# Destinations of the expert rows made by POOL, one instruction a tile, in a routed-expert kernel

## The chip, the cores and the metric

The kernel runs on one core of one Trainium2 chip. The metric is the device time of one launch in microseconds. Three runs of the kernel before gave 370.55, 370.05 and 370.35 us, a median of 370.35 us.

## What is computed

Four residual layers act on `x` (4 x 512 tokens of 128 values): a cross-attention to a small context, a layer of eight experts that each pick tokens, a second cross-attention, and a gated layer of eight SwiGLU experts with a shared expert beside them. The change is in the last one:

```
logits = normed @ router_w.T
top_v, top_i = top_k(softmax(logits), 2)          # two experts a token
gates = softmax(top_v)
out = sum over e of comb[:, e] * swiglu(normed, gate_up_w[e], down_w[e])
out = out + swiglu(normed, shared_gate_up_w, shared_down_w)
```

Each of the 2048 tokens goes to two different experts: 4096 rows of expert output.

## The kernel before, in words

**Sending.** When the router has chosen, POOL scatters each token's row twice into the DRAM table `dispatched_rows` (`send_rows`, L783 to L788, 32 indirect DMAs of 128 rows), once into the region of each of its two experts. A row is the normed token as high and low float16 halves, and three more words (L952, L953, L1016): word D is twice the token's number, word D+1 is its first expert, word D+2 is 0. SP writes pad rows behind the last row of each region: word D is 4096 + p (p is the partition), D+1 is -1, D+2 is 1.

**Tiles.** DVE plans 40 tiles of 128 slots. An expert takes as many tiles as its rows fill, the last one filled up with pad rows; tiles that no expert needs read the region of pads alone. So 40 x 128 = 5120 slots hold 4096 rows and 1024 pads. As the eight experts can need at most 39 tiles, the last tile holds pads only. `te` holds each tile's expert.

**The loop over tiles** is software-pipelined over PE, ACT, DVE, POOL and SP. At step s (`step_pe`, L1453; `step_act`, L669; `step_dve`, L1093):

- SP (`load_slots`, L471) loads tile n's rows into `slot_rows` (`xd`), a ring of four: the load of tile n waits until tile n-4 has been transposed (`rows_turned`) and until the destinations of tile n-4 have been taken out of its rows (`dest_ready`).
- PE transposes the rows of tile s+4 (L1462), multiplies tile s+3 with the gate and up weights (L1160, from `slot_rows_t`), transposes the hidden values of tile s+1 (L1482) and multiplies tile s with the down weights (L1160, from `region_x`), in this order.
- ACT makes the high half of tile s+2, the silu of tile s+3 and copies the turned hidden values of tile s+1 (L676, L681, L686).
- DVE makes `dbase` of tile s+4 (L1100), scales tile s-1's output into `yv`, a ring of four, and casts its destinations to int32 (L1108, L1110; the cast signals `rows_ready`), copies tile s+4's turned rows (L1115), makes the low half of tile s+2 (L1118), the destinations `dall` of tile s+4 (L1123, signals `dest_ready`), and the hidden values of tile s+3 (L1128).
- POOL (L807 to L815) waits for `rows_ready` of a tile and scatters its 128 output rows into the DRAM table `expert_rows` by an indirect DMA (L814). Its loop has a register for the value that is waited for.

The destination of a row is twice the token's number, plus 1 if this tile's expert isn't the token's first. Pads get rows of their own behind row 4096, other ones for each tile, which nothing reads.

**After the loop** SP waits for all scatters (L484), loads `expert_rows` in four parts into `region_q` (L487), and DVE, ACT and POOL add the two gated rows of each token to `x`, which SP stores. The shared expert's other half runs on PE, ACT and DVE between.

The lines that set the order around the change:

```python
            def load_slots(s, r):
                wait(eng, rows_turned, s - 3)
                wait(eng, dest_ready, s - 3)
                row = eng.value_load(trow_i[0:1, ds(s, 1)], min_val=0, max_val=E * REG)
                eng.dma_start(xd[:, r, :], disp[ds(row, P), :]).then_inc(rows_loaded[r], 16)
```

Of the kernel before, what the change touches and what calls it, by code (L numbers as in the profile page):

```python
# [14 lines left out]
ds = bass.ds  # L15
# [78 lines left out]
def build(nc, x_in, ctx_in, mask_in, gx_in, gf_in, wq0_in, wkv0_in, wr0_in, wv0_in, wo0_in, wk1_in,  # L94
          wq1_in, wv1_in, wo1_in, gamma_in, beta_in, router_in, wbig_in, c32_in, c16_in, cbf_in,
          pad_in, out):
    disp = nc.dram_tensor("dispatched_rows", ((E + 1) * REG, PAY_W), F32).ap()
    ytok = nc.dram_tensor("expert_rows", (2 * B * S + TILES * P + 1, D), F32).ap()
    x_v = x_in.rearrange("b (t p) d -> p (b t) d", p=P)
    out_v = out.rearrange("b (t p) d -> p (b t) d", p=P)  # L100
    ytok_v = ytok[0:2 * B * S, :].rearrange("(n p k) d -> p n (k d)", p=P, k=2)
# [1 line left out]
    with ExitStack() as ctx:  # L103
        def sb(name, shape, dt=F32):
            return ctx.enter_context(nc.sbuf_tensor(name, shape, dt))
# [146 lines left out]
        hs = region_w[:, 0:4 * CH].rearrange("p (r n) -> p r n", r=4)  # L252
        hsp = region_k[:, 0:2, :].bitcast(F16)
        xd = sb("slot_rows", [P, 4, PAY_W])
        dbase = sb("slot_dest_base", [P, 1])
        dall = sb("slot_dest_of", [P, TILES])
        dst = sb("slot_dest", [P, 4], I32)
        xdt = sb("slot_rows_t", [P, 2, 2 * P], F16)
        sil = region_w[:, 0:2 * FF].rearrange("p (r n) -> p r n", r=2)
        hid = region_w[:, 2 * FF:4 * FF].rearrange("p (r n) -> p r n", r=2)  # L260
# [139 lines left out]

        rows_loaded = [sem(f"rows_loaded{r}") for r in range(4)]
        dest_ready = sem("dest_ready")
        dest_base = sem("dest_base")
        rows_turned = sem("rows_turned")
        rows_turned_out = sem("rows_turned_out")
        gate_up_made = sem("gate_up_made")
# [302 lines left out]
        def _(pool):  # L709
# [94 lines left out]
                    send_rows(b, range(T // 2, T))  # L804


            due = pool.alloc_register("tiles_due")  # L807
            pool.reg_mov(due, 1)
            with pool.Fori(0, TILES // 4):
                for r in range(4):  # L810

                    pool.wait_ge(rows_ready, due)
                    pool.reg_add(due, due, 1)
                    pool.indirect_dma_start(ytok, bass.IndirectOffsetOnAxis(dst[:, r:r + 1].bitcast(U32), 0),  # L814
                                            yv[:, r, :], None).then_inc(rows_sent[r], 16)  # L815

            pool.wait_ge(sh_added, B)
            n = slice((B - 1) * T, NT)
# [7 lines left out]
        def _(dve):  # L826
# [127 lines left out]
            for stage, t in skewed(NT, C_EVERY, C_DVE):  # L954
# [34 lines left out]
                elif stage == "affine" and t % T == T - 1:  # L989
                    dve.wait_ge(ffn_normed, b + 1)  # L990
                    link(dve.tensor_tensor(xh[:, n, :], xh[:, n, :],
                                           gamma[:, :].rearrange("p (a d) -> p a d", a=1).to_broadcast((P, T, D)), ALU.mult))
                    dve.tensor_tensor(xh[:, n, :], xh[:, n, :],
                                      beta[:, :].rearrange("p (a d) -> p a d", a=1).to_broadcast((P, T, D)),
                                      ALU.add).then_inc(ffn_affine, 1)
                elif stage == "low" and t % T == T - 1:

                    dve.wait_ge(ffn_high, b + 1)
                    dve.tensor_tensor(pay[:, n, D // 2:D].bitcast(F16), xh[:, n, :], pay[:, n, 0:D // 2].bitcast(F16),
                                      ALU.subtract).then_inc(ffn_low, 1)  # L1000
                elif stage == "shift_logits" and t % T == T - 1:
                    l3 = bank[6][:, 0:T * E].rearrange("p (t e) -> p t e", e=E)
                    dve.wait_ge(route_logits, b + 1)
                    link(dve.tensor_reduce(rmax[:, :], l3, AX.X, ALU.max, negate=True))
                    dve.tensor_tensor(prob[:, n, :], l3, bc(rmax[:, :], E), ALU.add).then_inc(route_shifted, 1)
                elif stage == "route" and t % T == T - 1:

                    dve.wait_ge(route_exp, b + 1)
                    for u in range(b * T, (b + 1) * T):
                        last = dve.max(rtop[:, u, :], prob[:, u, :])  # L1010
                    link(last)
                    for u in range(T):
                        last = dve.max_index(ridx[:, u, :], rtop[:, b * T + u, :], prob[:, b * T + u, :])
                    link(last)
                    link(dve.tensor_copy(ef[:, :, :], ridx[:, :, 0:2]))
                    dve.tensor_copy(pay[:, n, D + 1], ef[:, :, 0])  # L1016
                    link(dve.tensor_tensor(oh[:, :, :, :].rearrange("p t c e -> p (t c) e"),
                                           c32[:, C_I8:C_I8 + E].rearrange("p (a e) -> p a e", a=1).to_broadcast((P, 2 * T, E)),
                                           bc(ef[:, :, :].rearrange("p t c -> p (t c)"), E), ALU.is_equal))
                    link(dve.tensor_tensor(msel[:, n, :], oh[:, :, 0, :], oh[:, :, 1, :], ALU.add))  # L1020
                    link(dve.tensor_reduce(tsum[:, :], msel[:, n, :].rearrange("p t e -> p e t"), AX.X, ALU.add))
                    dve.tensor_tensor(base[:, b + 1, :], base[:, b, :], tsum[:, :], ALU.add).then_inc(routed_marked, 1)
                elif stage == "slots" and t % T == T - 1:
                    if b == B - 1:

                        link(dve.tensor_reduce(rsum[:, :], prob[:, :, :], AX.X, ALU.add))
                        link(dve.reciprocal(rsum[:, :], rsum[:, :]))
                        link(dve.tensor_tensor(ptop[:, :, :], rtop[:, :, 0:2], bc(rsum[:, :], 2), ALU.mult))
                        dve.tensor_tensor(gexp[:, :], ptop[:, :, 1], ptop[:, :, 0], ALU.subtract).then_inc(top2_difference, 1)

                    dve.wait_ge(route_ranks, b + 1)
                    link(dve.tensor_tensor(rk[:, :, :], bank[7][:, 0:T * E].rearrange("p (t e) -> p t e", e=E),
                                           c32[:, C_EREG:C_EREG + E].rearrange("p (a e) -> p a e", a=1).to_broadcast((P, T, E)),
                                           ALU.add))
                    for c in range(2):
                        last = dve.tensor_tensor(ohr[:, :, c, :], oh[:, :, c, :], rk[:, :, :], ALU.mult)
                    link(last)
                    link(dve.tensor_reduce(slotf[:, :, :], ohr[:, :, :, :], AX.X, ALU.add))
                    dve.tensor_copy(slot[:, n, :], slotf[:, :, :]).then_inc(slots_ready, 1)
# [53 lines left out]
            def step_dve(s, u):  # L1093

                static = isinstance(s, int)
                if not static or 0 <= s + 4 < TILES:

                    dve.wait_ge(rows_loaded[u], (s + 4 - u) * 4 + 16)
                    wait(dve, dest_ready, s + 4)
                    dve.scalar_tensor_tensor(dbase[:, :], xd[:, u, D + 2:D + 3], c32[:, ds(C_S128 + s + 4, 1)],  # L1100
                                             xd[:, u, D:D + 1], ALU.mult, ALU.add).then_inc(dest_base, 1)
                if not static or 0 <= s - 1 < TILES:
                    r = (u - 1) % 4
                    dve.wait_ge(down_made, s)
                    if not static or s - 1 >= 4:

                        dve.wait_ge(rows_sent[r], (s - 1 - r) * 4)
                    dve.tensor_scalar(yv[:, r, :], bank[6 + r % 2][:, 0:D], 1.0 / WS, None, ALU.mult)  # L1108
                    dve.wait_ge(dest_ready, s)
                    dve.tensor_copy(dst[:, r:r + 1], dall[:, ds(s - 1, 1)]).then_inc(rows_ready, 1)  # L1110
                if not static or 0 <= s + 4 < TILES:

                    dve.wait_ge(rows_turned, s + 5)
                    wait(dve, gate_up_made, s + 3)
                    dve.tensor_copy(xdt[:, u % 2, :], xt_ps).then_inc(rows_turned_out, 1)  # L1115
                if not static or 0 <= s + 2 < TILES:
                    dve.wait_ge(hidden_high, s + 3)
                    dve.tensor_tensor(hsplit[:, u % 2, FF:2 * FF], hid[:, u % 2, :], hsplit[:, u % 2, 0:FF],  # L1118
                                      ALU.subtract).then_inc(hidden_low, 1)
                if not static or 0 <= s + 4 < TILES:  # L1120

                    dve.wait_ge(dest_base, s + 5)
                    dve.scalar_tensor_tensor(dall[:, ds(s + 4, 1)], xd[:, u, D + 1:D + 2], te[:, ds(s + 4, 1)],  # L1123
                                             dbase[:, :], ALU.not_equal, ALU.add).then_inc(dest_ready, 1)
                if not static or 0 <= s + 3 < TILES:
                    v = (u + 3) % 2
                    dve.wait_ge(silu_done, s + 4)
                    dve.scalar_tensor_tensor(hid[:, v, :], bank[2 * v + 1][:, 0:FF], 1.0 / WS, sil[:, v, :],  # L1128
                                             ALU.mult, ALU.mult).then_inc(hidden_done, 1)
# [471 lines left out]
```

## Time and profile before

| | us |
|---|---|
| three runs | 370.55, 370.05, 370.35 |
| span of the profiled execution, first to last instruction | 368.7 |
| steady part of the tile loop | about 258 to 338 |
| after the loop, to the end of the span | about 342 to 368.7 |

The time of the profiled execution itself isn't given apart from the three; by these, launch and end lie 1.4 to 1.9 us around its span, 1.65 us by the median. The profile was taken on the one core. Times in the rows are microseconds from the span's start. PE is TensorE (PEld its weight loads), DVE VectorE, ACT ScalarE, POOL GpSimd, SP the engine that only issues DMAs here. In a timeline a row has its start, its duration, the engine, the line and the tiles written and read; the end of a row of the same engine can lie a little behind the next one's start, because instructions overlap. The duration of an indirect DMA on POOL is the time in which POOL makes its descriptors; the data land later.

### The profile page before, as it was taken

To read this page: it belongs to the slowest core of one execution; us is meant where nothing else is said; L and a number is where in the kernel's file an instruction comes from. 1 tells how busy PE (TensorE), PEld (TensorE's weight loads), DVE (VectorE), ACT (ScalarE), POOL (GpSimd) and SP (SyncE) were. 2 spreads that over 40 slices of the span, in tenths; PEclk is the share of its full clock that TensorE was granted. 3 is DMA by queue.
4 is the path that set the end of the run, shared out by engine and by line. 5 is a ranking of instruction groups with operands and counts; after the bars stand their busy time and mean duration, and the time that the engine had idled before them with its cause. 6 is when DMAs were issued, how large, how long until landed. Compare 5 with 4: busy or idle time off the path is not lost.

```text
span 368.7 us, 7937 instructions
## 1 busy us (share of the span) xinstructions
PE 274.0 (74%) x2143; PEld 202.4 (55%) x2144; DVE 251.1 (68%) x884; ACT 213.6 (58%) x503; POOL 151.1 (41%) x201
## 2 busy tenths in 40 slices
PE   3499880395899876899897862536999999999810
PEld 2398780153677554577575751223776676776510
DVE  3256259996577631778889966833988788887475
ACT  1555549775577595845763534301877777777430
POOL 2412358960222510811732677760344444444502
PEclk9999996589899968999898855655999999999975
DMA  7860000620000000000000011221222122221173
GB/s 187 272 260 0 3 0 9 221 93 0 3 1 2 1 2 0 3 0 2 0 3 7 32 52 44 88 75 44 53 59 63 54 58 58 58 58 36 46 239 103
DMA packets 19469, 21.06 MB, mean 57 GB/s; under 512 B 3184, under 2 KB 17008, under 8 KB 18800
## 3 DMA queue, kind: packets, MB, share of 16 engines
q1 hardware_dynamic: 16992, 15.79, 14.1%
q0 software_dynamic: 2304, 4.77, 4.0%
q8 instruction: 14, 0.23, 0.3%
q10 hardware_dynamic: 144, 0.15, 0.2%
q14 instruction: 15, 0.12, 0.1%
HBM read 14.28 MB, written 6.42 MB: 56 GB/s over the span
## 4 chain that ended last, share of the span: by engine, by line
PE 54%; DVE 18%; issue 7%; POOL 7%; DMA 5%; ACT 5%; SPq 2%; DVEq 0%; POOLq 0%; ACTq 0%
PE bank L1160 43%; POOL dispatched_rows L787 5%; PE bank L1482 3%; DVE x L1151 2%; DMA region_q<-expert_rows 2%; DMA wr<-in 2%; DVE region_k L883 2%; PE bank L1462 2%; DVE region_k L967 2%; DVE top L882 2%; DVE nm L965 1%; ACT x_hat L514 1%; PE bank L1213 1%; PE bank L1196 1%; DVE bn_raw L838 1%
## 5 line engine op out<-in xcount | busy, mean ns | idle before, releaser
L814 POOL DMA_INDIRECT expert_rows<-region_k,slot_dest x40 | 38.2, 955 | 63.3 <-DVE slot_dest L1110 62.4
L1160 PE MATMUL bank<-w_high,slot_rows_t 128*128 x160 | 47.2, 337 | 3.2 <-issue 1.9
L681 ACT ACTIVATE region_w<-bank 128x384 f32<-128x384 f32 x40 | 19.6, 490 | 35.6 <-PE bank L1160 34.8
L787 POOL DMA_INDIRECT dispatched_rows<-region_t,slot x32 | 31.9, 997 | 16.1 <-issue 9.2
L1160 PE MATMUL bank<-w_high,region_x 128*128 (+1 forms) x272 | 35.8, 228 | 2.3 <-DVE region_t L908 2.1
L1128 DVE SCALAR_TENSOR_TENSOR region_w<-bank,region_w 128x384 f32<-128x384 f32 x40 | 22.3, 557 | 16.4 <-ACT region_w L681 15.3
L686 ACT ACTIVATE region_x<-bank 128x768 f16<-128x768 f16 x40 | 32.2, 804 | 0.9 <-PE bank L1482 0.9
L729 POOL TENSOR_SCALAR minus_mean_rstd<-mean_var 128x4 f32<-128x4 f32 x16 | 3.4, 213 | 71.1 <-DVE mean_var L841 45.7
L740 POOL TENSOR_TENSOR w_low<-w_scaled,w_high 128x512 f16<-128x512 f32 (+1 forms) x23 | 29.0, 1286 | 0.0
L514 ACT ACTIVATE x_hat<-x,minus_mean_rstd,rstd 128x128 f32<-128x128 f32 x64 | 26.2, 482 | 4.4 <-POOL minus_mean_rstd L732 4.4
L1160 PE MATMUL bank<-w_low,region_x 128*128 (+1 forms) x136 | 27.1, 227 | 0.0
L1160 PE MATMUL bank<-w_low,slot_rows_t 128*128 x80 | 26.9, 336 | 0.0
L1160 PEld LDWEIGHTS bank<-w_high,region_x 128*128 128x128 f16 x272 | 23.7, 98 | 3.2 <-issue 2.6
L1160 PEld LDWEIGHTS bank<-w_high,slot_rows_t 128*128 128x128 f16 x160 | 16.0, 100 | 14.4 <-issue 8.6
L1118 DVE TENSOR_TENSOR region_k<-region_w,region_k 128x384 f16<-128x384 f32 x40 | 22.3, 557 | 1.5 <-ACT region_k L676 1.4
L772 POOL TENSOR_TENSOR region_w<-region_k,rope_b 128x128 f32<-128x128 f32 x16 | 7.4, 463 | 36.4 <-DVE rope_b L926 36.4
L676 ACT ACTIVATE region_k<-region_w 128x384 f16<-128x384 f32 x40 | 20.9, 523 | 1.6 <-DVE region_w L1128 1.2
L1482 PE MATMUL bank<-c,region_k 128*128 128x128 f16 x240 | 19.9, 219 | 0.7 <-ACT region_x L686 0.7
L1482 PEld LDWEIGHTS bank<-c,region_k 128*128 128x128 f16 x240 | 16.6, 98 | 5.9 <-issue 1.0
L1160 PEld LDWEIGHTS bank<-v_blocks,region_k 128*128 128x128 f32 x128 | 17.9, 216 | 3.1 <-ACT region_k L631 1.7
L1160 PE MATMUL bank<-v_blocks,region_k 128*128 128x36 f32 x128 | 18.5, 295 | 0.8 <-DVE region_x L976 0.7
L634 ACT ACTIVATE region_k<-region_k 128x512 f32<-128x512 f32 x16 | 10.0, 628 | 15.6 <-DVE region_k L967 15.6
(238 smaller groups left out, 785.0 us busy)
## 6 DMA issues: line engine op xcount, KB each, us to landing
w_scaled<-in SPq DMA_DIRECT2D x5, 1024.0 KB, 8.2
slot_rows<-dispatched_rows SPq DMA_DIRECT2D x40, 65.5 KB, 1.9
region_q<-expert_rows SPq DMA_DIRECT2D x4, 512.0 KB, 5.7
x<-in SPq DMA_DIRECT2D x4, 256.0 KB, 4.4
region_w<-in SPq DMA_DIRECT2D x2, 512.0 KB, 6.9
out<-x SPq DMA_DIRECT2D x4, 256.0 KB, 2.6
w_scaled<-in SPq DMA_DIRECT2D x1, 704.0 KB, 4.0
expert_rows<-region_k,slot_dest POOLq DMA_INDIRECT x40, 2.2
```

Of the source, the lines that this page charges most:

```text
L514: last = act.activation(xh[:, t, :], x[:, t, :], ACT.Identity, bias=nmr[:, t:t + 1], scale=rstd[:, t:t + 1])
L634: act.activation(e1[:, t % 2, :], e1[:, t % 2, :], ACT.Exp, scale=HD ** -0.5).then_inc(cross1_exp, 1)
L676: act.activation(hsplit[:, u % 2, 0:FF], hid[:, u % 2, :], ACT.Copy).then_inc(hidden_high, 1)
L681: act.activation(sil[:, v, :], bank[2 * v][:, 0:FF], ACT.Silu, scale=1.0 / WS).then_inc(silu_done, 1)
L686: act.activation(hidt[:, (u + 1) % 2, :], ht_ps, ACT.Copy).then_inc(hidden_turned_out, 1)
L740: pool.tensor_tensor(wl[:, c], wf[:, r], wh[:, c], ALU.subtract).then_inc(w_low_done, 1)
L787: pool.indirect_dma_start(disp, bass.IndirectOffsetOnAxis(slot[:, b * T + t, c:c + 1].bitcast(U32), 0), pay[:, b * T + t, :], None).then_i ...
L814: pool.indirect_dma_start(ytok, bass.IndirectOffsetOnAxis(dst[:, r:r + 1].bitcast(U32), 0), yv[:, r, :], None).then_inc(rows_sent[r], 16)
L1118: dve.tensor_tensor(hsplit[:, u % 2, FF:2 * FF], hid[:, u % 2, :], hsplit[:, u % 2, 0:FF], ALU.subtract).then_inc(hidden_low, 1)
L1128: dve.scalar_tensor_tensor(hid[:, v, :], bank[2 * v + 1][:, 0:FF], 1.0 / WS, sil[:, v, :], ALU.mult, ALU.mult).then_inc(hidden_done, 1)
L1160: return pe.matmul(o, l, r, start=start, stop=stop)
L1482: last = pe.transpose(ht_ps[:, i * P:(i + 1) * P], hsplit[:, (u + 1) % 2, i * P:(i + 1) * P], ident16)
```

## The change

- POOL makes the destinations: `slot_dest(n)` waits for the load of tile n and writes `dst[:, n]`, now int32 and 40 columns wide, as (word D+1 equals the tile's expert) + word D, and signals `dest_ready`. DVE's three instructions L1100, L1110 and L1123 go, and `rows_ready` is signalled by L1108.
- Word D+1 of a sent row is the token's second expert in place of its first, so that "equal" adds the 1.
- Pads, whose destination is 4096 + p, are beyond the bound of the scatter and are skipped; `expert_rows` shrinks to 4096 rows.
- POOL's loop is unrolled. The destinations of tiles 0 and 1 are made ahead of it, those of tile n+2 at the head of iteration n, behind the scatter of tile n-1 and ahead of the wait for tile n's output.
- `load_slots` on SP is unchanged.

```diff
-            due = pool.alloc_register("tiles_due")
-            pool.reg_mov(due, 1)
-            with pool.Fori(0, TILES // 4):
-                for r in range(4):
-
-                    pool.wait_ge(rows_ready, due)
-                    pool.reg_add(due, due, 1)
-                    pool.indirect_dma_start(ytok, bass.IndirectOffsetOnAxis(dst[:, r:r + 1].bitcast(U32), 0),
-                                            yv[:, r, :], None).then_inc(rows_sent[r], 16)
+            def slot_dest(n):
+
+                pool.wait_ge(rows_loaded[n % 4], n // 4 * 16 + 16)
+                pool.tensor_scalar(dst[:, n:n + 1], xd[:, n % 4, D + 1:D + 2], te[:, n:n + 1], xd[:, n % 4, D:D + 1],
+                                   ALU.is_equal, ALU.add).then_inc(dest_ready, 1)
+
+            slot_dest(0)
+            slot_dest(1)
+            for n in range(TILES):
+                if n + 2 < TILES:
+                    slot_dest(n + 2)
+                pool.wait_ge(rows_ready, n + 1)
+                pool.wait_ge(dest_ready, n + 1)
+                pool.indirect_dma_start(ytok, bass.IndirectOffsetOnAxis(dst[:, n:n + 1].bitcast(U32), 0),
+                                        yv[:, n % 4, :], None, bounds_check=2 * B * S - 1, oob_is_err=False).then_inc(rows_sent[n % 4], 16)
...
-                    dve.tensor_copy(pay[:, n, D + 1], ef[:, :, 0])
+                    dve.tensor_copy(pay[:, n, D + 1], ef[:, :, 1])
...
-                if not static or 0 <= s + 4 < TILES:
-
-                    dve.wait_ge(rows_loaded[u], (s + 4 - u) * 4 + 16)
-                    wait(dve, dest_ready, s + 4)
-                    dve.scalar_tensor_tensor(dbase[:, :], xd[:, u, D + 2:D + 3], c32[:, ds(C_S128 + s + 4, 1)],
-                                             xd[:, u, D:D + 1], ALU.mult, ALU.add).then_inc(dest_base, 1)
...
-                    dve.tensor_scalar(yv[:, r, :], bank[6 + r % 2][:, 0:D], 1.0 / WS, None, ALU.mult)
-                    dve.wait_ge(dest_ready, s)
-                    dve.tensor_copy(dst[:, r:r + 1], dall[:, ds(s - 1, 1)]).then_inc(rows_ready, 1)
+                    dve.tensor_scalar(yv[:, r, :], bank[6 + r % 2][:, 0:D], 1.0 / WS, None, ALU.mult).then_inc(rows_ready, 1)
...
-                if not static or 0 <= s + 4 < TILES:
-
-                    dve.wait_ge(dest_base, s + 5)
-                    dve.scalar_tensor_tensor(dall[:, ds(s + 4, 1)], xd[:, u, D + 1:D + 2], te[:, ds(s + 4, 1)],
-                                             dbase[:, :], ALU.not_equal, ALU.add).then_inc(dest_ready, 1)
```

## Rows read from the trace of the kernel before

**Rows 1.** Busy time by stretch, here the tile loop's; columns: PE, PEld, DVE, ACT, POOL, clock

```profile
258.60:337.90 79.30, 74.17 (x806) 56.05 (x805) 65.13 (x246) 58.32 (x107) 32.48 (x34) 1.00 0.21 57
```

**Rows 2.** Who waited for whom, 255 to 342 us: total, times, longest

```profile
PEld bank L1160 <- issue: 8.4, 31, 0.4
...
PE bank L1160 <- DVE region_w L1128: 0.9, 5, 0.2
```

**Rows 3.** SP's own waits over the span, and line L476's landings

```profile
SPq L424 <- DVE slot_dest_of L1123: 26.2, 29, 1.5
...
DMA to landing us min/median/max: 1.8/1.9/2.7
```

**Rows 4.** Timeline of the loop: transposes, DVE's small steps, loads and a scatter

```profile
282.53 0.28 PE L1462 MATMUL bank<-c,slot_rows 128*128 128x128 f16 x2
285.04 0.27 PE L1462 MATMUL bank<-c,slot_rows 128*128 128x128 f16 x2
285.13 0.34 SPq L476 DMA_DIRECT2D slot_rows<-dispatched_rows  x1
285.40 0.29 DVE L1108 TENSOR_SCALAR region_k<-bank 128x128 f32<-128x128 f32 x1
286.41 0.21 DVE L1123 SCALAR_TENSOR_TENSOR slot_dest_of<-slot_rows,tile_expert,slot_dest_base 128x1 f32 x1
287.29 0.28 PE L1462 MATMUL bank<-c,slot_rows 128*128 128x128 f16 x2
287.50 0.34 SPq L476 DMA_DIRECT2D slot_rows<-dispatched_rows  x1
287.73 0.21 DVE L1100 SCALAR_TENSOR_TENSOR slot_dest_base<-slot_rows,c 128x1 f32<-128x1 f32 x1
287.85 0.28 DVE L1108 TENSOR_SCALAR region_k<-bank 128x128 f32<-128x128 f32 x1
288.97 0.96 POOL L814 DMA_INDIRECT expert_rows<-region_k,slot_dest  x1 [1.49 <-DVE slot_dest L1110]
289.78 0.28 DVE L1108 TENSOR_SCALAR region_k<-bank 128x128 f32<-128x128 f32 x1
292.02 0.28 PE L1462 MATMUL bank<-c,slot_rows 128*128 128x128 f16 x2
```

**Rows 5.** Timeline of POOL in straight-line code, and what DVE did ahead

```profile
200.33 0.17 DVE L1039 CAST slot<-slot_f 128x8 int32<-128x8 f32 x1
200.81 1.22 POOL L787 DMA_INDIRECT dispatched_rows<-region_t,slot  x1 [6.90 <-DVE slot L1039]
...
219.77 0.19 POOL L729 TENSOR_SCALAR minus_mean_rstd<-mean_var 128x4 f32<-128x4 f32 x1 [0.23 <-DVE mean_var L987]
```

**Rows 6.** Lines L729 and L814: ns least, median, most; L814's landings

```profile
L729 POOL TENSOR_SCALAR minus_mean_rstd<-mean_var x16: 190/193/520, 5.6 to 219.8; 128x4 f32<-128x4 f32 x16
...
L814 POOL DMA_INDIRECT expert_rows<-region_k,slot_dest x40: 952/955/959, 262.6 to 348.0; - x40
...
DMA to landing us min/median/max: 2.2/2.2/3.0
```

**Rows 7.** Timeline: tile 0's output, and the transposes of tiles 7, 37, 39

```profile
261.46 0.28 DVE L1108 TENSOR_SCALAR region_k<-bank 128x128 f32<-128x128 f32 x1
264.78 0.28 PE L1462 MATMUL bank<-c,slot_rows 128*128 128x128 f16 x2
333.18 0.28 PE L1462 MATMUL bank<-c,slot_rows 128*128 128x128 f16 x2
337.89 0.28 PE L1462 MATMUL bank<-c,slot_rows 128*128 128x128 f16 x2
```

**Rows 8.** Timeline: a scatter begun beside DVE's L1118

```profile
341.05 0.56 DVE L1118 TENSOR_TENSOR region_k<-region_w,region_k 128x384 f16<-128x384 f32 x1 [0.33 <-ACT region_k L676]
341.49 0.95 POOL L814 DMA_INDIRECT expert_rows<-region_k,slot_dest  x1 [1.03 <-DVE slot_dest L1110]
```

**Rows 9.** The chain that ended last, the last scatter: start, length, what

```profile
348.02 3.12 DMA expert_rows<-region_k,slot_dest
```

More of the change, by code:

```diff
@@ L97, in build @@
     disp = nc.dram_tensor("dispatched_rows", ((E + 1) * REG, PAY_W), F32).ap()
-    ytok = nc.dram_tensor("expert_rows", (2 * B * S + TILES * P + 1, D), F32).ap()
+    ytok = nc.dram_tensor("expert_rows", (2 * B * S, D), F32).ap()
     x_v = x_in.rearrange("b (t p) d -> p (b t) d", p=P)
@@ L254, in build @@
         xd = sb("slot_rows", [P, 4, PAY_W])
-        dbase = sb("slot_dest_base", [P, 1])
-        dall = sb("slot_dest_of", [P, TILES])
-        dst = sb("slot_dest", [P, 4], I32)
+        dst = sb("slot_dest", [P, TILES], I32)
         xdt = sb("slot_rows_t", [P, 2, 2 * P], F16)
@@ L402, in build @@
         dest_ready = sem("dest_ready")
-        dest_base = sem("dest_base")
         rows_turned = sem("rows_turned")
```

## The prediction

> **What bounds the kernel now.** I read the stretches first. In the steady tile loop, 258.6 to 337.9 us, PE is busy 74.2 of 79.3 us at a granted clock of 1.00, DVE 65.1, ACT 58.3 and POOL 32.5 [rows 1]. PE sets the pace; DVE, from which the change takes work, is full but not first. The waits say the same: in the loop PE waited for DVE in 5 places, 0.9 us in all, while its other gaps, the largest group of them 8.4 us ahead of weight loads, have no other engine as releaser: they are its own sequencer's [rows 2]. Then SP's waits: 29 times it waits for DVE's L1123, the signal `dest_ready`, before it loads a tile [rows 3]. That wait costs nothing today, but the change moves its producer. Last, the chain that ended last: after the loop it runs through POOL's last scatters and the landing of the last one [rows 9].
>
> **Removed from DVE.** L1100, L1110 and L1123 go; the first and the last take 0.21 us each a tile [rows 4]. What they can give back in the loop is bounded by PE's 0.9 us of waits for DVE [rows 2]; I cost it at nothing there, since PE's own work hides it. One thing counts below: L1100, started at 287.73, was ahead of L1108 at 287.85 [rows 4]; without it L1108 starts 0.12 us sooner. The column that the router's code writes is another one of the same size: nothing.
>
> **Moved: `dest_ready`.** Call T(n) the transposes of tile n. Today L1123 for tile n runs 1.4 us behind T(n) (286.41 behind 285.04), and lets the load into that slot, that of tile n+4, be issued at 287.50. There is room: the load that T at 292.02 used was issued at 285.13, three steps earlier, and landed by 287.0; 5.0 us to spare [rows 4]. After the change the destinations of tile n come from POOL, behind the scatter of tile n-3. The output of the tile whose down product is in the step of T at 285.04 is scattered from 288.97 to 289.93, and only behind that can POOL make the destinations that free the load for T at 292.02 [rows 4]. From 289.93 to the landing it takes some 3 us. So a ring of dependences closes that was open: T(n) -> down product of tile n-4, in the same step -> L1108 -> scatter of n-4 on POOL -> `slot_dest(n-1)` -> SP loads tile n+3 -> T(n+3), three steps later. Its length:
>
> - T(n) to the end of L1108: 282.53 to 285.69, 285.04 to 288.13 and 287.29 to 290.06 [rows 4] are 3.16, 3.09 and 2.77, mean 3.01; less 0.12: 2.89. Ends: 2.65 and 3.04.
> - End of L1108 to the end of the scatter: today 1.80 us (288.13 to 289.93), with a cast and a loop's register between. In straight-line code, from a signal at 200.50 to the end of a DMA at 202.03, it was 1.53 [rows 5]. I take 1.53, as the new code is straight-line; 1.80 is the other end.
> - POOL from there to `slot_dest`: an op behind a DMA began 0.23 us after it, with a wait for DVE in that [rows 5]. At least nothing, at most 0.23; I take 0.15.
> - `slot_dest`: the nearest row is POOL's TENSOR_SCALAR of 128x4, 190 to 520 ns, median 193 [rows 6]. I take 0.19 and keep 0.52 as the end.
> - Its signal to SP's DMA: from 286.62 to 287.50, 0.88 [rows 4].
> - Load to landing: 1.8 least, 1.9 median, 2.7 most [rows 3]. I take 1.9; a longer one is rare.
>
> Sum 2.89 + 1.53 + 0.15 + 0.19 + 0.88 + 1.90 = 7.54 us for three tiles. Today T(7) at 264.78 to T(39) at 337.89 [rows 7] is 73.1 us for 32 tiles, 6.85 for three. The ring is longer by 0.7 us, so it becomes the bound, and PE's own gaps are spent inside the wait for the load.
>
> The first tile that feels it is 7, since `slot_dest` of 0 to 2 stands behind no scatter. L1108 of tile 0, at 261.46 today [rows 7], starts 0.12 sooner and ends at 261.62; plus 1.53, 0.34, 0.88 and 1.9 gives T(7) at 266.3, today 264.8. Ten rounds of 7.54 lead to T(37) at 341.7, today 333.2. Two tiles on, with no wait among them, at 2.2 us each (the shorter step in rows 4 is 2.25), T(39) stands at 346.1 against 337.9: **+8.2 us**.
>
> Queues: SP's holds only loads in the loop, one each 2.5 us, 0.34 us to issue [rows 4]. POOL's holds 1.3 us for a scatter and 0.35 for `slot_dest` a tile, within 2.5; the new wait for `rows_loaded` costs it nothing, because that tile has been transposed by then. Behind it on POOL waits only the next scatter, whose output isn't ready yet.
>
> **After the loop.** The chain goes through POOL's scatters, back to back, and the last one lands 3.12 us after its start at 348.02 [rows 9], whereas the median landing is 2.2 [rows 6]. Straight-line code ends the chain 0.2 us sooner. The last tile holds pads only and is skipped whole: its landing may fall by 0 to 0.9 us; I take 0.4. Together -0.6. Whether skipped rows save time on POOL no row shows. A fifth of the slots are pads, so -0.19 us of 0.955 [rows 6] is the lower end; the longest indirect DMA, 1.22 us [rows 5], gives +0.26 for the bound check as the upper; I take 0, as 40 scatters of mixed content took 952 to 959 ns [rows 6].
>
> By the Trainium skill (DMA: Bandwidth & Descriptors, "Anatomy of one DMA — SWDGE (gpsimd) path") the fixed part of a DMA, about 2 us, is mostly the wait until the target memory confirms the write; a scatter that writes nothing would then gain all of the 0.9, and the tail would be -1.1.
>
> Sum 8.2 - 0.6 = +7.6, so a span of 376.3 us; the runs' median lies 1.65 us above the span of the profile, and with that the time is 378.0 us.
>
> **Rivals.**
>
> *A, faster: the loads still come in time, 368.9 us.* Every tile's load is the place, and 6.85 us the point: a ring shorter than that never binds. What stays then is PE's 0.9 us of waits for DVE [rows 2] and half of the tail's 0.6 to 1.1, 1.5 us in all. For it: the ring exceeds the point by 10% only, and is a sum of six terms. Against it: with all at their least (2.65, 1.34, 0, 0.19, 0.88, 1.8) it is 6.86.
>
> *B, `slot_dest` is held up by DVE, 383.6 us.* L1118 reads two tiles of SBUF for 0.56 us a step [rows 8]. If POOL's small op stood behind it each time, a round would be 8.1 us, ten of them 5.6 more. For it: a TENSOR_SCALAR on POOL took up to 520 ns beside a median of 193 [rows 6]. Against it: the scatter at 341.49 began while L1118 ran from 341.05, and took its usual 0.95 [rows 8].
>
> The Trainium skill (SBUF — State Buffer, "SBUF: two separate sides") has the ports that VectorE and GpSimd share as an exclusive lock, which a VectorE op with two SBUF inputs takes against a GpSimd op that reads SBUF. It speaks for B; no row here shows such a lock on a small op for certain.
>
> *C, the bound check makes each scatter dearer, 380.6 us:* 0.26 us a round, ten rounds.
>
> *D, no difference, 370.3 us.* The ring binds at tile 7 alone (+1.5), and later tiles catch up, because PE's gaps in the rest of the loop are larger than in the steps read here, and tail and DVE give 1.5 back.
>
> **Chances.** Forecast 0.65, B 0.12, C 0.08, A 0.10, D 0.05. Under 0.2% (0.7 us) a measurement can't be told from no change. Slower is 0.65 + 0.12 + 0.08 = 0.85, faster 0.10, the same 0.05. The range: POOL's wake at 1.80 and `slot_dest` at 0.52 lengthen a round by 0.6, which is +6; a scatter 0.19 shorter, no gap behind it and a landing of 1.8 shorten it by 0.44, which is -4.4, with -0.5 more from the tail. So 373 to 384, which holds C and B and leaves out A and D.
>
> **What would show it.** Right: L1462 waits for the DMA of `slot_rows`, about once in three tiles; these transposes come 7.5 us apart in threes; SP waits for POOL's new line in place of L1123, and issues about 0.9 us behind it; DVE is less busy in the loop by over 15 us, with no gain from it. Wrong: no such waits and an even 2.28 us a tile (A); POOL's new op at 0.5 us or more, or starting at the end of L1118 (B); scatters of over 1.1 us (C).

## The result, and the profile after

The changed kernel takes 385.63 us (median of 4, 383.19 to 387.48) against 370.2 us; the ratio is 1.0399 with a 95% interval of 1.0337 to 1.046. It is slower, on the side that was forecast, but by about twice as much: 378.0 was predicted and 373 to 384 given as the range. An execution over 1.5% above the fastest of its kernel is left out of every ratio below; here there was none.

The profiled execution has a span of 385.2 us. First the tile loop, T(4) to T(39), in the view of busy time by stretch (stretch, length, PE, PEld, DVE, ACT, POOL, clock, DMA share, GB/s); it answers to [rows 1]:

```profile
261.10:355.30 94.20, 77.90 (x806) 56.15 (x807) 54.70 (x142) 59.09 (x108) 51.49 (x68) 1.00 0.17 45
```

From T(4) to T(39) it is 94.2 us where it was 79.5, for the same 806 matmuls at the same granted clock. DVE has 10.4 us less to do, POOL 19.0 more, and no engine is busy throughout. So a wait sets the pace. Who waited for whom, 255 to 360 us (total, times, longest), and then SP's own waits, which answer to [rows 2, 3]:

```profile
PE bank L1452 <- DMA slot_rows<-dispatched_rows: 11.2, 22, 1.5
...
PEld bank L1452 <- DMA slot_rows<-dispatched_rows: 7.0, 9, 1.7
...
POOL expert_rows L817 <- POOL slot_dest L807: 4.6, 7, 0.8
```

```profile
SPq L421 <- POOL slot_dest L807: 49.2, 33, 6.4
```

L1452 are the transposes (L1462 before). They now wait for their rows, which they did only at the start of the loop before; and SP waits for POOL's `slot_dest`, no longer for DVE. At first the wait is long and comes every third tile, as forecast: PE idles 1.52 us ahead of T(7), 1.20 ahead of T(10) and 1.05 ahead of T(13). From T(16) on it is spread over nearly all tiles, mostly 0.1 to 0.6 us each, because there are three such rings, one for every third tile, and each sets the time of its own tiles. One round of the ring, from a timeline of 300 to 311 us; it answers to [rows 4]:

```profile
301.20 0.28 PE L1452 MATMUL bank<-c,slot_rows 128*128 128x128 f16 x2 [0.38 <-DMA slot_rows<-dispatched_rows]
...
303.82 0.29 DVE L1105 TENSOR_SCALAR region_k<-bank 128x128 f32<-128x128 f32 x1
...
304.89 1.18 POOL L817 DMA_INDIRECT expert_rows<-region_k,slot_dest  x1 [1.25 <-DVE region_k L1105]
...
306.12 0.38 POOL L807 TENSOR_SCALAR slot_dest<-slot_rows,tile_expert 128x1 int32<-128x1 f32 x1
...
307.38 0.34 SPq L473 DMA_DIRECT2D slot_rows<-dispatched_rows  x1
...
309.38 0.28 PE L1452 MATMUL bank<-c,slot_rows 128*128 128x128 f16 x2 [0.58 <-DMA slot_rows<-dispatched_rows]
```

The lines show the whole ring. T(19) is at 301.20, L1105 stores the output of tile 15 until 304.11, its scatter ends at 306.07, the destinations of tile 18 are made by 306.50, the load of tile 22 is issued 0.88 us later, and T(22) is at 309.38, 8.18 us after the start. The durations of all 40, in ns (least, median, most), against [rows 6]:

```profile
L807 POOL TENSOR_SCALAR slot_dest<-slot_rows,tile_expert x40: 367/378/389, 254.3 to 362.2; 128x1 int32<-128x1 f32 x40
...
L817 POOL DMA_INDIRECT expert_rows<-region_k,slot_dest x40: 974/1112/1338, 265.0 to 365.6; - x40
```

And the chain that ended last, its longest pieces where it goes into the tail, against [rows 9]:

```profile
358.95 1.11 POOL expert_rows L817
361.04 0.98 POOL expert_rows L817
362.75 0.89 POOL expert_rows L817
364.56 1.07 issue
365.62 2.15 DMA expert_rows<-region_k,slot_dest
```

The last scatter lands 2.15 us after its start instead of 3.12. The 16.5 us between the two spans lie here:

| stretch | before | after | difference |
|---|---|---|---|
| start to T(4) | 258.4 | 261.1 | +2.7 |
| T(4) to T(7) | 6.4 | 8.2 | +1.8 |
| T(7) to T(37), ten rounds | 68.4 | 80.4 | +12.0 |
| T(37) to T(39) | 4.7 | 5.6 | +0.9 |
| T(39) to the end | 30.8 | 29.9 | -0.9 |

The first row is not the change's, as far as the other profiles tell: T(4) stood at 261.5 in a kernel with none of the change's new dependences (e10 below), at 256.8 in the three-ahead version of the change, and at 259.7 in the changed kernel's second profile. From 130 to 220 us the granted clock was 0.82 in this profile and 0.84 before. Without this row the change costs 13.8 us, 3.7%, inside the interval.

### The profile page after: what moved, and what is told of

It is laid out like the page before. It is cut to its first block, busy times and chain, and to the rows that moved or that the text cites. A ratio compares the mean times of both kernels' runs of the same rounds, so it can differ in the third digit from the quotient of the medians.

```text
span 385.2 us, 7759 instructions
## 1 busy us (share of the span) xinstructions
PE 280.9 (73%) x2143; PEld 205.4 (53%) x2144; DVE 238.7 (62%) x764; ACT 213.6 (55%) x503; POOL 173.1 (45%) x241
## 4 chain that ended last, share of the span: by engine, by line
PE 41%; DVE 16%; POOL 11%; issue 10%; DMA 9%; ACT 7%; SPq 3%; DVEq 0%; POOLq 0%; ACTq 0%
PE bank L1150 33%; DMA slot_rows<-dispatched_rows 6%; POOL dispatched_rows L784 5%; POOL expert_rows L817 4%; DVE x L1141 2%; SPq L472 2%; DMA region_q<-expert_rows 2%; DVE region_k L886 2%; DVE top L885 1%; ACT region_w L678 1%; POOL slot_dest L807 1%; DVE region_k L970 1%; DVE nm L968 1%; PE bank L1354 1%; PE bank L1452 1%
## 5 line engine op out<-in xcount | busy, mean ns | idle before, releaser
L817 POOL DMA_INDIRECT expert_rows<-region_k,slot_dest x40 | 44.9, 1123 | 48.8 <-DVE region_k L1105 41.0
L1118 DVE SCALAR_TENSOR_TENSOR region_w<-bank,region_w 128x384 f32<-128x384 f32 x40 | 22.3, 557 | 32.7 <-ACT region_w L678 32.7
L1113 DVE TENSOR_TENSOR region_k<-region_w,region_k 128x384 f16<-128x384 f32 x40 | 22.4, 559 | 4.9 <-ACT region_k L673 4.0
L1452 PE MATMUL bank<-c,slot_rows 128*128 128x128 f16 x80 | 11.6, 229 | 18.9 <-DMA slot_rows<-dispatched_rows 18.3
L1110 DVE COPY slot_rows_t<-bank 128x256 f16<-128x256 f16 x40 | 11.5, 289 | 14.6 <-PE bank L1452 14.3
L1150 PEld LDWEIGHTS bank<-v_blocks,region_k 128*128 128x128 f32 x128 | 19.1, 227 | 2.6 <-ACT region_k L628 1.7
L1150 PE MATMUL bank<-v_blocks,region_k 128*128 128x36 f32 x128 | 19.5, 305 | 0.4 <-DVE region_x L979 0.3
```

The source lines that it names most:

```text
L1150: return pe.matmul(o, l, r, start=start, stop=stop)
L1452: last = pe.transpose(xt_ps[:, h * P:(h + 1) * P], w, ident16)
```

## The experiments

The theory is the ring of the prediction, which allows three tiles a turn. Its rivals are that the small op itself on POOL slows the loop (by its own time or by holding up DVE), that the unrolled code does, or that the bound check does. In the table, loop is T(7) to T(39), the rest T(39) to the end of the span, in us. Each ratio is to executions of the kernel before that were taken beside that kernel's own; their medians were 370.2, 370.67 and 370.54 us.

| kernel | loop | rest | time | ratio to before |
|---|---|---|---|---|
| before | 73.1 | 30.8 | 370.2 | |
| after | 86.0 | 29.9 | 385.63 | 1.0399 |
| e1_lead3 | 73.3 | 29.8 | 370.38 | 0.9995 (0.9957 to 1.0033) |
| e8_lead4 | 73.1 | 29.8 | 369.37 | 0.9959 (0.9919 to 0.9999) |
| e2_lead1 | 144.6 | 30.5 | 447.35, one run | |
| e7_doubled | 91.3 | 30.2 | 393.41 | 1.0584 (1.0496 to 1.0671) |
| e5_dve_one | 73.0 | 29.6 | 370.82 | 0.9975 (0.9938 to 1.0011) |
| e6_unrolled | 73.1 | 29.9 | 368.13, one run | |
| e3_before_bound | 73.1 | 30.4 | 369.97, one run | |
| e4_between | 73.1 | 30.5 | 369.73, one run | |
| e9_two_waits | 73.1 | 30.3 | 369.81, one run | |
| e10_unrolled_bound | 73.1 | 30.5 | 373.37, one run | |
| after_again | 85.8 | 29.9 | 385.86, one run | |

**Three tiles ahead (e1_lead3).**

```diff
-            slot_dest(0)
-            slot_dest(1)
+            for n in range(3):
+                slot_dest(n)
...
-                if n + 2 < TILES:
-                    slot_dest(n + 2)
+                if n + 3 < TILES:
+                    slot_dest(n + 3)
```

> The changed kernel with its destinations made three tiles ahead instead of two, nothing else. Theory (the ring: T(n), down product, L1105, scatter, slot_dest, load, T(n+3), 8.04 us a round in the changed kernel): the same chain now leads to T(n+4), so it asks for 8.04/4 = 2.01 us a tile, less than the 2.28 that PE needs by itself. T(7) to T(37) falls from 80.4 to about 68.4 us as in the kernel before, no waits of the transposes for slot_rows, time 368.5 to 370.5. Rival 1 (POOL's small op and the DVE it shares ports with slow the loop): the op is still there 40 times, so the time stays above 378. Rival 2 (unrolled POOL code or the bound check costs the loop): likewise above 375.

370.38 us, and T(7) at 263.33, T(37) at 331.98: 68.65 us. The op still runs 40 times for 0.38 us, the code is as unrolled, the bound is there; the 12 us of the ten rounds are gone. This shows the ring and refutes all three rivals as the cause of these 12 us. Its POOL from 262 to 344 us, by line (count, busy, mean ns, idle before and its releasers):

```profile
L817 POOL DMA_INDIRECT expert_rows<-region_k,slot_dest x37 | 41.4, 1120 | 26.1 <-DVE region_k L1105 14.6 <-POOL slot_dest L807 10.9 <-issue 0.6
L807 POOL TENSOR_SCALAR slot_dest<-slot_rows,tile_expert 128x1 int32<-128x1 f32 x36 | 13.6, 379 | 1.9
```

POOL has the same instructions as in the changed kernel, of the same mean lengths (1123 and 379 ns there); only the place of `slot_dest` differs.

**One tile ahead (e2_lead1).** The same lines with 1 in place of 3.

> The changed kernel with the destinations made one tile ahead instead of two. Ring theory: the chain of 8.04 us now leads to T(n+2), 4.02 us a tile: T(7) to T(37) 120.6 us instead of 80.4, time about 385.6 + 40 + 3 = 429. Rivals (the op's own cost on POOL or DVE): the same number of ops, so 383 to 388.

The direction and the scale hold, 447.35 us, but T(7) to T(37) is 134.9 us, 14 more than expected: 8.99 us a round of two tiles, not 8.04. The view of the stretch has a lower granted clock, and the two steps from T(22) and T(23) show where it acts:

```profile
270.00:390.00 120.00, 76.42 (x629) 54.36 (x626) 41.79 (x110) 46.31 (x83) 39.14 (x54) 0.83 0.10 27
338.89:342.93 4.04, 3.95 (x28) 2.62 (x29) 1.59 (x5) 1.28 (x3) 0.12 (x1) 0.62 0.11 33
342.45:345.03 2.58, 2.08 (x26) 1.52 (x23) 1.96 (x6) 2.21 (x5) 1.26 (x2) 1.00 0.00 0
```

PE idled 2.4 to 3.6 us ahead of the transposes of every even tile, T(6) to T(38). Behind 15 of these 17 gaps the granted clock from the transposes to the end of L1105 was 0.50 to 0.71 on the mean, between its two levels of 1.2 and 2.4 GHz; behind the other two, of 3.14 and 3.25 us, it was 1.00. In the loops of the kernels above it was 1.00. From T to the end of L1105 it took 4.04 us in the step shown and 3.94 on the mean of the even tiles, where the changed kernel takes 2.91. The rounds between odd tiles lose their time elsewhere: T to the end of L1105 is 2.93 there, but from the issue of the load to the transposes it is 2.95 us, against 1.91, because PE is still in the slow step of the even tile when the rows are there. POOL's steps and the issue of the load took as long as in the changed kernel, but for scatters that were about 0.06 us shorter. So the ring's law is confirmed, and its length isn't a constant: the part of it that PE does grew where the granted clock was lower.

**The op twice (e7_doubled).**

```diff
+                pool.tensor_scalar(dst2[:, n:n + 1], xd[:, n % 4, D + 1:D + 2], te[:, n:n + 1], xd[:, n % 4, D:D + 1],
+                                   ALU.is_equal, ALU.add)
                 pool.tensor_scalar(dst[:, n:n + 1], xd[:, n % 4, D + 1:D + 2], te[:, n:n + 1], xd[:, n % 4, D:D + 1],
```

> The changed kernel with a second POOL instruction of the same form ahead of each slot_dest, its result unused. Ring theory: 0.38 us more in a round of three tiles, 0.4 with the gap: T(7) to T(37) 84.3 instead of 80.4, time 389 to 390. If the op stood aside of the ring: no change, 385.6. If POOL's small op blocked DVE's: more than 0.4 a tile, over 395.

393.41 us, T(7) to T(37) 86.2: 0.58 us more a round. POOL by line, 270 to 357 us, and the landings of SP's loads:

```profile
L820 POOL DMA_INDIRECT expert_rows<-region_k,slot_dest x30 | 35.2, 1173 | 27.5 <-DVE region_k L1108 21.2 <-POOL slot_dest L810 6.3
L808 POOL TENSOR_SCALAR slot_dest_again<-slot_rows,tile_expert 128x1 int32<-128x1 f32 x31 | 12.2, 393 | 1.6
L810 POOL TENSOR_SCALAR slot_dest<-slot_rows,tile_expert 128x1 int32<-128x1 f32 x31 | 11.1, 359 | 0.0
...
DMA to landing us min/median/max: 1.7/1.8/3.0
```

Added up over the ten rounds T(7) to T(37), the 5.8 us are 3.6 of the second op, 1.7 between the issue of a load and its transposes, 0.4 of longer scatters (1173 ns on the mean, 1123 in the changed kernel) and 0.1 of PE's part. Of the 1.7, 1.0 stand in one round, T(13) to T(16): the loads of tiles 11, 12 and 15 took 2.5 to 3.0 us to land, where none took over 1.9 in the changed kernel's first profile, and the rows of tile 16, landed after 1.89 us, had to wait for PE. Why those loads were late is open. The op is on the ring, and by itself it costs what the ring says, 0.36 us a round; the expected size was missed by a third, by the loads in the main.

**The op on DVE (e5_dve_one).**

```diff
-            def slot_dest(n):
...
+                if not static or 0 <= s + 4 < TILES:
+
+                    dve.wait_ge(rows_loaded[u], (s + 4 - u) * 4 + 16)
+                    dve.tensor_scalar(dst[:, ds(s + 4, 1)], xd[:, u, D + 1:D + 2], te[:, ds(s + 4, 1)], xd[:, u, D:D + 1],
+                                      ALU.is_equal, ALU.add).then_inc(dest_ready, 1)
```

> The changed kernel with the one instruction (same formula, int32 output) on DVE, in the place of the first of the three of before, and not on POOL; second expert sent, pads skipped, POOL loop unrolled as in the change. Ring theory: dest_ready is again early, no ring; DVE is lighter by two small instructions, worth little because PE is first: loop as before or up to 1 us shorter, tail 0.5 to 1 us shorter, time 368.5 to 370. Rival (the bound check or the unrolled loop costs): above 373.

370.82 us, 0.8 above the expected 368.5 to 370, ratio 0.9975: no difference from the kernel before that can be told. Everything of the change is in it but the engine of the op: second expert sent, one instruction in place of three, pads skipped, loop unrolled. Together these parts cost nothing that can be told, and their gain is within the noise. It also has the scatter with a bound and nothing in front of it on POOL:

```profile
292.64 0.98 POOL L807 DMA_INDIRECT expert_rows<-region_k,slot_dest  x1 [0.89 <-DVE region_k L1100]
294.30 0.28 DVE L1100 TENSOR_SCALAR region_k<-bank 128x128 f32<-128x128 f32 x1
295.36 0.98 POOL L807 DMA_INDIRECT expert_rows<-region_k,slot_dest  x1 [1.73 <-DVE region_k L1100]
```

From the signal at 294.58 to the end at 296.34 it is 1.76 us; the prediction had 1.53, the changed kernel has 1.96 in the round shown above and 1.89 in the commoner case (298.69 to 300.58). The next five kernels take that way apart, since it is the largest part of what was missed. None of them has a ring, and all have a loop of 73.1 us. Their times missed the expected 369 to 371 us (370 to 371 for e6_unrolled) twice, 368.13 in e6_unrolled and 373.37 in e10_unrolled_bound; the loops are alike, and most of that difference stands ahead of T(4), at 256.9 and 261.5 us.

**POOL's loop unrolled, in the kernel before (e6_unrolled).**

```diff
-            with pool.Fori(0, TILES // 4):
-                for r in range(4):
...
+            for n in range(TILES):
+                pool.wait_ge(rows_ready, n + 1)
+                pool.indirect_dma_start(ytok, bass.IndirectOffsetOnAxis(dst[:, n % 4:n % 4 + 1].bitcast(U32), 0),
+                                        yv[:, n % 4, :], None).then_inc(rows_sent[n % 4], 16)
```

> The kernel before with POOL's loop over the scatters unrolled, nothing else (three DVE instructions, no bound check). It asks whether straight-line code shortens the way from the signal to the end of a scatter from today's 1.73 us behind the cast to the 1.53 that the prediction took. Prediction's term right: the scatter starts about 0.3 to 0.6 us behind the cast's end and takes 0.95 to 1.2. Rival (the form of the code doesn't matter, an idle POOL needs 0.77 us): start 0.77 behind, 0.955 long, as before. Time 370 to 371 either way.

```profile
293.45 0.14 DVE L1105 CAST slot_dest<-slot_dest_of 128x1 int32 x1
...
293.87 1.30 POOL L809 DMA_INDIRECT expert_rows<-region_k,slot_dest  x1 [0.95 <-DVE slot_dest L1105]
```

The scatter starts 0.28 us behind the cast and is 1.3 us long: 1.58 in sum, against 1.73 in the loop form. Five of the 40 took 1.23 in sum. So the prediction's 1.53 was close for straight-line code without a bound.

**The bound alone, in the kernel before (e3_before_bound)**, and **both (e10_unrolled_bound)**. The edit, in POOL's loop of before and of e6_unrolled:

```diff
-                                            yv[:, r, :], None).then_inc(rows_sent[r], 16)
+                                            yv[:, r, :], None, bounds_check=2 * B * S - 1, oob_is_err=False).then_inc(rows_sent[r], 16)
```

> The kernel before with the bound check on its scatters, so that its pad rows are skipped, nothing else. Theory now: the bound check is not what made a scatter 1.11 us long in the changed kernel; here it stays at 0.96 to 0.99 us. Rival C of the prediction (the check costs): 1.1 us or more. Time 369 to 371; if the skipped rows shorten the last landing, the last scatter lands under 2.5 us after its start instead of 3.1.

> e6_unrolled with the bound check, one wait. If the bound makes the difference of 0.17 us: the scatter starts 0.7 to 0.85 behind the cast and is 0.98 long, 1.76 in sum; if the second wait does: 1.59 to 1.62 in sum. Time 369 to 371 either way.

e3_before_bound, with one of its scatters, and then e10_unrolled_bound:

```profile
L814 POOL DMA_INDIRECT expert_rows<-region_k,slot_dest x40: 982/982/994, 262.5 to 348.0; - x40
...
289.77 0.14 DVE L1110 CAST slot_dest<-slot_dest_of 128x1 int32 x1
...
290.75 0.98 POOL L814 DMA_INDIRECT expert_rows<-region_k,slot_dest  x1 [0.88 <-DVE slot_dest L1110]
```

```profile
291.16 0.15 DVE L1105 CAST slot_dest<-slot_dest_of 128x1 int32 x1
...
292.08 0.98 POOL L809 DMA_INDIRECT expert_rows<-region_k,slot_dest  x1 [1.47 <-DVE slot_dest L1105]
```

In the loop form the duration hardly changes, 982 ns for 955; the start moves too, from 0.77 us behind the cast to 0.84 by the median (0.83 to 0.94 for most), and the sum from 1.73 to 1.83. In straight-line code, which the changed kernel has, the scatter with the bound begins 0.77 us behind the cast instead of 0.28 and is 0.98 long instead of 1.31: the duration falls, and the sum rises by 0.17 to 1.75. The durations alone would have acquitted the bound check in one form and made it a gain in the other. The 40 DMAs take 982 to 994 ns, whether none, some or all of their rows are skipped, so skipping makes POOL's part no shorter. The last scatter of e3_before_bound landed 2.69 us behind its start; under 2.5 was expected if skipping shortens the landing.

**A second wait, in e6_unrolled (e9_two_waits).**

```diff
                 pool.wait_ge(rows_ready, n + 1)
+                pool.wait_ge(dest_ready, n + 1)
```

> e6_unrolled with a second wait, on dest_ready, between the wait for rows_ready and the scatter; it is met long before. From the signal to the end of a scatter e6_unrolled took 1.59 us (start 0.28 behind the cast, 1.31 long), and the changed kernel's form with a bound and two waits 1.76 (start 0.78, 0.98 long, in e5_dve_one). If the second wait makes the difference: start 0.7 to 0.8 behind the cast and 0.95 long here. If the bound does: 0.28 and 1.31 as in e6_unrolled. Time 369 to 371 either way.

```profile
292.52 0.15 DVE L1106 CAST slot_dest<-slot_dest_of 128x1 int32 x1
...
292.94 1.31 POOL L810 DMA_INDIRECT expert_rows<-region_k,slot_dest  x1 [1.39 <-DVE slot_dest L1106]
```

0.27 and 1.31 us, as without it. The second wait is free; the 0.17 us are the bound's.

**A small op in front of each scatter, in e6_unrolled (e4_between).**

```diff
+                pool.tensor_scalar(dst2[:, n:n + 1], trow[:, n:n + 1], te[:, n:n + 1], tb[:, n:n + 1],
+                                   ALU.is_equal, ALU.add)
                 pool.wait_ge(rows_ready, n + 1)
```

> e6_unrolled with one small POOL TENSOR_SCALAR of slot_dest's form ahead of every scatter, on data that nothing waits for; no bound check, destinations still by DVE. Theory: an indirect DMA that follows a compute instruction on POOL takes 1.06 to 1.2 us instead of 0.955, whatever the check; the op takes 0.38. As POOL is outside any ring here, the time stays at 370 to 371. Rival C: without a check the scatters stay at 0.955.

```profile
L813 POOL DMA_INDIRECT expert_rows<-region_k,slot_dest x40: 1058/1405/1430, 261.6 to 347.6; - x40
```

The edit also has one wait ahead of the loop. Against the unrolled form's 1310 ns by the median it is 1405: 0.1 us more, with no bound anywhere. The start stays at 0.28 us behind the cast by the median, and the sum goes from 1.59 to 1.69. The expectation compared with the 0.955 of the loop form and so gave a number that is off (1.06 to 1.2); its point, that the op in front lengthens the scatter, holds. With a bound the same step is from 0.98 to 1.11.

**Four ahead (e8_lead4)**, the lines of e1_lead3 with 4.

> The changed kernel with its destinations made four tiles ahead instead of two. Ring theory: at three ahead nothing of the ring was left, so a fourth gives nothing more: loop T(7) to T(37) 68.4 to 68.8 us, time within 0.5% of the kernel before. If a rest of the ring still cost something at three (SP waited 33.6 us for slot_dest there), the loop is shorter here by 0.5 us or more.

369.37 us; T(7) to T(37) 68.4, against 68.65 at three ahead. So at three ahead some 0.2 us of the ring is left at most. The ratio's interval ends at 0.9999, which puts this version at the edge of being told from the kernel before: its loop is the same length and the rest of its span 1 us shorter, 0.3%. The intervals of the two leads overlap.

**The changed kernel again (after_again)**, no edit.

> The changed kernel once more, to see what of its time repeats. Ring theory: T(7) to T(37) within 0.3 us of 80.4, as the ring has nothing random in it; the time ahead of the loop differs by 1 to 3 us with the granted clock between 130 and 220 us. Time 383 to 387.5.

385.86 us. T(7) to T(37) is 80.6 (80.4 the first time), T(4) at 259.7 (261.1). The ring repeats; the part ahead of it is what varies.

## Why the prediction was right in kind and wrong in size

**The mechanism** held in its main points: which wait would close (`dest_ready` behind the scatter of tile n-3), from which tile on (T(7), 266.3 forecast; T(4) was 2.7 us later in this profile than before, and T(7) is at 269.3), that it spans three tiles, that SP would wait for POOL and issue 0.88 us behind it, and that DVE's relief would bring nothing. The three-ahead and one-ahead kernels show it. One point was too simple: the waits stood at every third tile only up to T(13), and at nearly every tile later, as all three rings bind.

**The size** of a round was forecast at 7.54 us and is 8.04. One sign of the prediction was off as well: DVE was to be less busy in the loop by over 15 us, and it is by 10.4. The three lines (L1100, L1110, L1123) were busy 7.4, 4.9 and 7.7 us in the loop before, but they overlap their neighbours, and the busy time counts the union. Term by term, in the round shown and on the mean of the ten rounds from T(7) to T(37):

| term | predicted | round shown | mean of ten |
|---|---|---|---|
| T(n) to the end of L1105 | 2.89 | 2.91 | 2.91 |
| signal to the end of the scatter | 1.53 | 1.96 | 1.91 |
| gap to `slot_dest` | 0.15 | 0.05 | 0.05 |
| `slot_dest` | 0.19 | 0.38 | 0.38 |
| signal to SP's DMA | 0.88 | 0.88 | 0.88 |
| load to the transposes | 1.90 | 2.00 | 1.91 |
| sum | 7.54 | 8.18 | 8.04 |

The step that failed is the pricing of POOL's two instructions in the sum of the ring: from the signal to the end of `slot_dest` it has 1.53 + 0.15 + 0.19 = 1.87 us, and the runs have 1.91 + 0.05 + 0.38 = 2.34, which is 0.47 of the 0.50 us by which a round was missed. In both instructions I took the low end where the row I read was not quite the same thing. For `slot_dest` the row was a TENSOR_SCALAR with constants (193 ns, [rows 6]); the new op takes three columns of SBUF as operands and writes int32, and costs 378. For the scatter I wrote that the bound check costs 0 and that straight-line code wakes in 1.53 us. The second is nearly true (1.58), the first isn't: 0.17 for the bound, hidden ahead of the DMA's start, and 0.13 because a compute op runs just before, which I hadn't listed. Rival C (the bound check makes each scatter dearer) was right in kind and at its 0.26 a little too high, but I had kept it apart from the forecast with a chance of 0.08. Its sign, scatters of over 1.1 us, did appear (1.11), and for another reason: with the bound alone they take 0.98, and the op in front makes the rest.

Ten rounds of 0.5 are 5.0 us of the 6.5 by which the loop was missed; 0.3 comes from the way to T(7), and 1.2 from the last two tiles, which I had put at PE's own pace with no wait (4.4 us). They took 5.57, more than the 4.71 of before, because the other two rings bind too: T(38) and T(39) waited for their loads like T(37). This is the second step that failed. The tail was -0.9 for -0.6.

**Rival A** (the loads come in time) needed a round under 6.85 and is refuted by the waits. **Rival B** (`slot_dest` held by DVE) is refuted as a cause: all 40 took 367 to 389 ns, and from T(7) to T(37) each began 0.05 us behind the scatter ahead of it, whatever DVE did. That its 8.1 us a round comes nearer to the measured 8.04 than the forecast does is luck. But what B describes exists, and strikes too seldom to matter. L1113, the op with two SBUF inputs (L1118 before), hardly ever ran when `slot_dest` began; in the second profile of the changed kernel (after_again) it did twice:

```profile
268.77 0.55 DVE L1113 TENSOR_TENSOR region_k<-region_w,region_k 128x384 f16<-128x384 f32 x1
...
269.06 0.50 POOL L807 TENSOR_SCALAR slot_dest<-slot_rows,tile_expert 128x1 int32<-128x1 f32 x1
```

This `slot_dest` took 502 ns and the other one 406, instead of 375, and in e7_doubled two `slot_dest_again` that began in the same way took 581 and 582. All four ended 0.24 to 0.25 us behind the end of DVE's instruction, which is what a wait for that end would look like. By the lock of the Trainium skill's page SBUF — State Buffer ("SBUF: two separate sides") the instruction that starts first keeps the shared ports for its whole length and the other one blocks. The four cases agree with that, and so do two more, in which the overlap was 3 and 26 ns and the op took its usual time, since it ended later than that anyway. Where the POOL op began first, by 0.2 to 0.4 us, DVE's kept its 557 to 559 ns, with overlaps of up to 0.17 us (e7_doubled), so no block of DVE by POOL shows here. Two of the four DVE instructions that began first, those in e7_doubled, took 736 and 697 ns; why is open.

**The skipped pads.** The last tile writes nothing, and its DMA landed 2.13 to 2.19 us after its start in both profiles of the changed kernel and in e1_lead3, e2_lead1, e5_dve_one, e7_doubled and e8_lead4; the kernels that write its pads had 2.69 to 3.17. But e3_before_bound and e10_unrolled_bound, which skip them too, had 2.69 and 2.86, so the 0.5 to 1 us isn't cleanly the skip's. The Trainium skill (DMA: Bandwidth & Descriptors, "Anatomy of one DMA — SWDGE (gpsimd) path") puts most of a DMA's fixed 2 us or so down to the receipt of the write in the target memory, by which a missing write could be the whole gain. These two runs speak against so simple a reading, and it stays open.

**The range** was too narrow above: it let one term be high while the others stayed at their taken values, 6 us in all. With the scatter at 1.80 + 0.26 and the op at 0.52, ends that the text itself named, a round would have been 0.86 longer and the range have reached 387.

## What to carry to other kernels

When the producer of a "buffer is free" signal moves to another engine, write down what stands ahead of it in that engine's queue, follow the signal round to where it starts, and divide the length by the number of tiles between. Here 8.04 us by 3 is 2.68 us a tile, slower than PE's 2.28; by 4 it is 2.01 and doesn't bind, and one character in the code (n + 2 or n + 3) decides 4% of the kernel's time. There are as many such rings as tiles between, and here all three came to bind. In such a ring every term counts in full, ten times over here, so price each from a row with the same operands and the same neighbours, and let the range add up the high ends rather than take them one at a time. Work taken from an engine that is busy but not first brought nothing in any form: 73.0 to 73.3 us of loop with three, one or no instructions on DVE.

## What the runs showed of the hardware that was not expected

- A bound on an indirect DMA of 128 rows in straight-line code costs 0.17 us on the way from the signal to its end, 1.58 to 1.75 us, though the DMA's duration falls from 1.31 to 0.98: it starts 0.77 us behind the signal instead of 0.28. In the loop form it costs 0.10, 1.73 to 1.83.
- A POOL compute op right ahead of an indirect DMA makes it 0.1 us longer (1310 to 1405 ns without a bound, 983 to 1112 with one).
- A POOL TENSOR_SCALAR on one column takes 378 ns with operands from SBUF and int32 output, where the 128x4 one with constants takes 193.
- A `slot_dest` that began while DVE's op with two SBUF inputs ran ended 0.24 to 0.25 us behind the end of that op and took up to 582 ns for its usual 378 (four cases, in after_again and e7_doubled); where it began first, neither was longer.
- TensorE's granted clock stayed at 1.00 in the changed kernel's loop, where PE idled up to 1.5 us ahead of the transposes, and averaged 0.83 where it idled 2.4 to 3.6 us at every second tile (e2_lead1); a round grew there by 0.95 us, 14 us in all.
